# A recommendation tower on one core: twelve one-hot tables instead of ten, and a new order of products and layers

## What is computed

```python
e = jnp.stack([tbl_0[ids[:, 0]], ..., tbl_25[ids[:, 25]]], axis=1)       # 512 x 26 x 128
combined = jnp.concatenate([dense[:, None, :], e], axis=1)              # 27 fields
interactions = jnp.einsum('bfd,bgd->bfg', combined, combined)
z = concatenate([dense, interactions[:, iu, ju]], axis=1)               # iu, ju: pairs f < g
h = concatenate([z, dense], axis=1)
h = maximum(h @ W_top1 + b_top1, 0)                                     # 607 -> 512
h = maximum(h @ W_top2 + b_top2, 0)                                     # 512 -> 256
y = h @ W_top3                                                          # 256 -> 1
```

## Time and profile before

| | |
|---|---|
| Median of 3 runs | 120.84 us (120.73 to 121.73) |
| Profiled execution | 121.33 us |
| its span in the profile | 119.5 us |
| PE busy | 97.4 us (81%) |
| DVE, ACT, POOL busy | 74.1, 71.6, 67.1 us |
| mean granted TensorE clock | 0.986 of full |

### The profile page before, as it was taken

How to read it: one execution, slowest core, us unless ns; L and a number is a source line. 1 busy time by engine, 2 the same in 40 slices (tenths; PEclk the granted TensorE clock), 3 DMA queues, 4 the chain that set the end, 5 groups by cost and what they waited for, 6 DMA issues and landing times.

```text
span 119.5 us, 3462 instructions
## 1 busy us (share of the span) xinstructions
PE 97.4 (81%) x1494; PEld 78.9 (66%) x1494; DVE 74.1 (62%) x112; ACT 71.6 (60%) x137; POOL 67.1 (56%) x71
## 2 busy tenths in 40 slices
PE   0359999998999899689774949979997796498991
PEld 0147787784776677467563838969887795497760
DVE  2599799899979979992020890793079305184210
ACT  5449799999999997952322860792089110195101
POOL 2777777878687777777777677776740000000000
PEclk9999999999999999999999999999999999959999
DMA  2999974769958779721212222221220000000000
GB/s 69 240 333 348 331 246 110 250 85 293 389 167 302 230 171 334 278 69 37 59 44 71 52 54 62 49 69 47 56 59 5 0 0 5 5 0 0 0 5 1
DMA packets 5829, 14.72 MB, mean 123 GB/s; under 512 B 1707, under 2 KB 1707, under 8 KB 5686
## 3 DMA queue, kind: packets, MB, share of 16 engines
q1 hardware_dynamic: 3746, 10.28, 27.3%
q0 software_dynamic: 2048, 4.20, 12.7%
q10 hardware_dynamic: 20, 0.02, 0.1%
HBM read 14.50 MB, written 0.00 MB: 121 GB/s over the span
## 4 chain that ended last, share of the span: by engine, by line
PE 68%; DVE 20%; issue 8%; ACT 2%; ACTq 1%; DVEq 0%
PE gram_ps L475 17%; PE gram_ps L477 16%; PE gram_ps L521 9%; PE h_ps L546 8%; DVE zT L389 7%; DVE zT L386 7%; PE fill_ps L498 5%; PE h_ps L488 3%; PE h_ps L566 3%; DVE table_lo L409 2%; DVE featT L380 2%; PE fill_ps L576 2%; PE gram_ps L546 1%; DVE onehot L403 1%; ACT L319 1%
## 5 line engine op out<-in xcount | busy, mean ns | idle before, releaser
L263 POOL DMA_INDIRECT gathered<-tbl,ids_sb x64 | 66.3, 1035 | 20.7 <-issue 18.9
L475 PE MATMUL gram_ps<-onehot,table_hi 128*128 128x512 f32 x80 | 33.6, 420 | 5.5 <-DVE table_lo L409 3.8
L403 DVE TENSOR_TENSOR onehot<-h_ps,rowno 128x3072 fp32r<-128x3072 f32 (+1 forms) x11 | 33.6, 3060 | 3.0 <-PE h_ps L488 3.0
L477 PE MATMUL gram_ps<-onehot,table_lo 128*128 128x512 f32 x80 | 32.6, 407 | 0.0
L475 PEld LDWEIGHTS gram_ps<-onehot,table_hi 128*128 128x128 f32 x80 | 16.0, 199 | 10.5 <-issue 3.9
L386 DVE COPY zT<-gram_ps 32x128 f32<-32x128 f32 x32 | 9.1, 283 | 17.2 <-PE gram_ps L521 16.3
L521 PE MATMUL gram_ps<-featT 128*32 128x27 f32 x1024 | 13.1, 195 | 7.3 <-issue 4.9
L293 ACT ACTIVATE zT<-gram_ps 32x128 f32<-32x128 f32 x32 | 8.6, 270 | 16.0 <-PE gram_ps L521 15.4
L477 PEld LDWEIGHTS gram_ps<-onehot,table_lo 128*128 128x128 f32 x80 | 15.9, 199 | 3.2
L546 PE MATMUL h_ps<-zT,w_inter_sb 128*128 128x128 f32 x112 | 14.7, 280 | 2.5 <-DVE zT L389 2.5
L521 PEld LDWEIGHTS gram_ps<-featT 128*32 128x32 f32 x1024 | 10.9, 110 | 8.5 <-issue 5.9
(11 more groups left out here) (38 smaller groups left out, 65.0 us busy)
## 6 DMA issues: line engine op xcount, KB each, us to landing
table_sb<-tbl SPq DMA_DIRECT2D x10, 512.0 KB, 5.6
ids_all<-oh_ids SPq DMA_DIRECT2D x10, 256.0 KB, 4.9
gathered<-tbl,ids_sb POOLq DMA_INDIRECT x64, 4.2
w_inter_sb<-w_inter SPq DMA_DIRECT2D x1, 1024.0 KB, 7.6
w_dense_sb<-w_dense SPq DMA_DIRECT2D x1, 512.0 KB, 5.9
w_sb<-w SPq DMA_DIRECT2D x1, 512.0 KB, 9.0
dense_sb<-dense SPq DMA_DIRECT2D x1, 256.0 KB, 7.6
ids_sb<-ids SPq DMA_DIRECT2D x1, 52.0 KB, 1.9
```

Source lines behind the costliest of these rows:

```text
L263: pool.indirect_dma_start(out=gathered[:, t % ROW_BUFS, pos - FIRST_GATHERED, :], out_offset=None, in_=tables[table], in_offset=bass.Indir ...
L403: nc.vector.tensor_tensor(onehot[:, k % 2, c0:c1, :], ids_ps(k).unsqueeze(1).to_broadcast(of_chunks), rowno[:, c0:c1].unsqueeze(2).to_broa ...
L475: nc.tensor.matmul(lookup_ps(k), table_hi[:, k % SPLIT_BUFS, rows], onehot[:, k % 2, c, :], start=(c == 0), stop=False)
L477: last = nc.tensor.matmul(lookup_ps(k), table_lo[:, k % SPLIT_BUFS, rows], onehot[:, k % 2, c, :], start=False, stop=(c == RCHUNKS - 1))
```

## The change

`ONEHOT_TABLES` gains tables 18 and 20, so there are 12 lookups and 14 gathered fields; groups of gathered fields have 4, 4, 4 and 2 members. Fills (1,2), (1,3), (2,0) and (2,1) are put behind lookups. Both layers of tile t use one bank: `h1_ps`, `h2_ps` and a fill bank for tiles 0, 1, 2. `h1` has two buffers. PE's order is new: products of all tiles first, with layer 1 of tiles 0 and 1 between them; then second layers of tiles 0 and 1 and the first of tile 2; then the last tile in halves of 64 samples. `BLOCK` puts the quarters of a tile that DVE and ACT copy first into the first half. The functions with `_half` are new, `hidden1_last_half` goes. The scores are written into `denseT`.

```diff
-ONEHOT_TABLES = (0, 1, 3, 6, 8, 11, 12, 14, 15, 16)
+ONEHOT_TABLES = (0, 1, 3, 6, 8, 11, 12, 14, 15, 16, 18, 20)
-GROUPS = [range(p, p + GROUP) for p in range(FIRST_GATHERED, FEATS, GROUP)]
+GROUPS = [range(p, min(p + GROUP, FEATS)) for p in range(FIRST_GATHERED, FEATS, GROUP)]
+BLOCK = (0, 2, 1, 3)
-AFTER_LOOKUP = [[], [(0, 0)], [(0, 1)], [(0, 2)], [(0, 3)], [(1, 0)], [(1, 1)], [], [], []]
+AFTER_LOOKUP = [[], [(0, 0)], [(0, 1)], [(0, 2)], [(0, 3)], [(1, 0)], [(1, 1)], [(1, 2)], [(1, 3)], [(2, 0)], [(2, 1)], []]
-        h1 = sb("h1", [P, N1, P])
+        h1 = sb("h1", [P, 2, N1, P])
+        def layer_ps(t):
+            return (h1_ps, h2_ps, fill_ps[0])[t]
+        def layer1_half_ps(half, n):
+            return product_ps(LAST - 1)[:, half * BANK + n * HALF:half * BANK + (n + 1) * HALF]
+        def layer2_half_ps(half, n):
+            return (fill_ps[1], h1_ps)[half][:, n * HALF:(n + 1) * HALF]
+            def layer1_half(half):
+                pe.wait_ge(z_dve, 2 * ZCOPIES * LAST + (half + 1) * ZCOPIES)
+                pe.wait_ge(z_act, 2 * ZCOPIES * LAST + (half + 1) * ZCOPIES)
+                b0 = LAST * P + half * HALF
+                for n in range(N1):
+                    for c in range(ZCHUNKS):
+                        last = nc.tensor.matmul(layer1_half_ps(half, n), w_inter_sb[:, c, n * P:(n + 1) * P],
+                                                zT[:, c, b0:b0 + HALF],
+                                                start=False, stop=(c == ZCHUNKS - 1), skip_group_check=True)
+                last.then_inc(h1_psum_half, 1)
+            def layer2_half(half):
+                if half == 0:
+                    fills_read(1)
+                    pe.wait_ge(h1_ready, N1 * (LAST + 1))
+                else:
+                    pe.wait_ge(h2_ready, N2)
+                    pe.wait_ge(h1_act, N1)
...
             def layer2(t):
-                if t > 0:
-                    pe.wait_ge(h2_ready, N2 * t)
...
+                pe.wait_ge(h1_ready, N1 * (t + 1))
```

The end of the vector engine's order, the last tile's part on it and the scores:

```diff
             hidden1(2)
-            products_to_zT(3, 0)
-            products_to_zT(3, 1)
-            hidden1(LAST)
-            scores(1, 0, LAST * P)
-            scores(0, LAST * P, P)
+            hidden1_first_half()
+            hidden2_first_half()
+            scores(0, 0, LAST * P)
+            scores(1, LAST * P, P)
```

More of the change, by code:

```diff
@@ L148, in tower @@
         h2_psum = sem("h2_psum")
+        h2_psum_half = sem("h2_psum_half")
+        h2_half_dve = sem("h2_half_dve")
+        h2_half_act = sem("h2_half_act")
         h2_ready = sem("h2_ready")
@@ L308, in hidden2 @@
                 for n in range(N2):
-                    nc.scalar.activation(h2[:, n, t * P:(t + 1) * P], h2_ps[:, n * P:(n + 1) * P], ACT.Relu,
+                    nc.scalar.activation(h2[:, n, t * P:(t + 1) * P], layer2_ps(t, n), ACT.Relu,
                                          bias=b2_sb[:, n:n + 1]).then_inc(h2_ready, 1)
@@ L556, in layer2, with layer3 @@
                     pe.wait_ge(w2_in, 16)
-                if t > 0:
-                    pe.wait_ge(h2_ready, N2 * t)
[L559 to L568, removed]
-                last.then_inc(h2_psum, 1)
[L571 to L574, removed]
+                pe.wait_ge(h1_ready, N1 * (t + 1))
+                for n in range(N2):
+                    for k in range(N1):
+                        last = nc.tensor.matmul(layer2_ps(t, n), w2_sb[:, k, n * P:(n + 1) * P],
+                                                h1[:, t % 2, k, :], start=(n == 0 and k == 0), stop=(k == N1 - 1),
+                                                skip_group_check=True)
+                last.then_inc(h2_psum, 1)
+            def layer3(part, first, count):
+                pe.wait_ge(h2_ready, N2 * LAST)
+                if part == 1:
+                    pe.wait_ge(h2_half_dve, N2)
+                    pe.wait_ge(h2_half_act, N2)
                 for k in range(N2):
-                    last = nc.tensor.matmul(fill_ps[bank][0:1, 0:count], w3_sb[:, k:k + 1], h2[:, k, first:first + count],
+                    last = nc.tensor.matmul(score_ps(part)[0:1, 0:count], w3_sb[:, k:k + 1], h2[:, k, first:first + count],
                                             start=(k == 0), stop=(k == N2 - 1))
@@ L628, in _ @@
                 layer1(2, n)
[L629 to L632, removed]
-            layer2(2)
[L634 to L639, removed]
+            layer2(1)
+            layer1_dense_half(0)
+            layer1_dense_half(1)
+            layer1_half(0)
+            layer1_half(1)
+            layer2(2)
+            layer2_half(0)
+            layer2_half(1)
+            layer3(0, 0, LAST * P)
+            layer3(1, LAST * P, P)
 def first_layer_layout(w1):
```

182 lines of the change are left out of this document (107 added, 75 removed).

## The result

| | before | after |
|---|---|---|
| Median of 4 runs | 121.09 us (120.73 to 121.73) | 126.23 us (125.16 to 126.61) |
| Profiled execution, its span | 121.33, 119.5 us | 126.37, 124.5 us |
| First product starts | 58.54 | 67.73 |
| Last product ends | 104.05 | 98.24 |
| Last copy ends | 117.96 | 122.93 |

The ratio is 1.040, with a 95% interval of 1.032 to 1.049. The forecast was 128.5 us in 122.0 to 131.0. Whatever the kernel, some executions are longer by a few per cent; the ratios and intervals here, and the mean of old12b, use only the others (two each for `again`, whole12b, old12b and new10b), while the traces of `again`, whole12b, whole12c and new10b are of longer ones.

A forecast was written before the change was run, and what follows sets the result against it. DVE was taken to pace the lookups, PE's work and idle time the rest. Lookups to 68.1, 31.8 to the last product, 25.9 after and 1.54 store gave 127.3 us span, 128.5 us forecast, range 122.0 to 131.0.

The forecast's parts named there:

- Direction and bound: Whole kernel: slower, chance 0.86; DVE paces the lookups, PE's work plus its idle time sets the second stage.
- the waits for copies: PE's second-stage waits for DVE and ACT copies, about 5.9 us, go; no new wait that PE meets.
- narrower range of 125.5 to 130.5: Forecast's own range: 3.3 to 3.8 us a block, half-width instruction 0.10 to 0.12, lookups 9.1 to 11.3; chance 0.67.
- cheap halves: Rival, last tile: a 64-column matmul with new weights takes about 0.06 us, 6.3 us go, 122.2 us; chance 0.09.
- Two lookups, +10.2 us: Lookup stage: one more pair at the distance of lookups 6 to 8, 10.15 us; bounds 9.1 to 11.3 us.
- Stalls, 7.7 us: PE's products: waits for instruction blocks total 7.7 us against 4.94 before; 5.9 to 9.0 us by time per block.
- the 6 to 9 us that the prediction named as its sign: Products: idle time ending by issue, five to seven times, 255 instructions from end to end, would show the prediction right.
- the blocks of the prediction: PE's instructions arrive in blocks of 254, 3.6 us from entry to next arrival; first boundary about 176 instructions into the products.
- Halves, +6.3 us: Last tile: 112 instructions of 64 columns at 0.116 us, 13.0 us, replace 56 of 128 at 0.12, 6.7 us.
- The sum: Span 127.3 us: lookups to 68.1, 31.8 to the last product, 25.9 after it, 1.54 for the store.
- Clock: Rival: two stretches of product stalls bring the lower clock, each costing 1.2 us or so, 131 us; chance 0.12.

The follow-up runs named there:

- again: The new kernel unchanged, run again on the same chip and in the same rounds as whole12c: ratio to before 1.038.
- whole12b: The new kernel with the halves undone, last tile whole through both layers in the second fill bank, on another chip: ratio to before 1.013.
- old12b: The kernel before with twelve one-hot tables, its order and whole last tile kept: 127.03 and 127.38 us, where before had 121.0 beside it.
- new10b: The new order with the ten tables of before, two h1 buffers and the last tile whole: 116.06 and 117.69 us, ratio to before 0.970.
- whole12c: The new kernel with the last tile whole, on the first chip at a later time, beside the unchanged new kernel: ratio to before 0.996.
- wide: The new kernel with each half of the last tile's first layer computing all 128 columns: 125.55 us, before beside it 120.43.
- twice: The new kernel with each product matmul issued twice into the same place, 2048 more matmuls and weight loads: 156.49 us.

## Why the prediction was right, step by step

**Direction and bound.** Right. PE's work and its stalls set the second stage, and the waits for copies went away as said, with none in their place. The size was not as good: the forecast was 7.7 us above before (128.5 against 120.84), and the measured difference is 5.1. The narrower range of 125.5 to 130.5 holds the time too. But the range as stated also took in cheap halves (122.2 us), so the time by itself does not show that the mechanism was right; the rows of the halves and of the stalls do.

**Two lookups, +10.2 us.** 9.2 us. The term was taken from a pair with a full fill behind one lookup; fill (1,3) has two transposes now, its copy took 0.42 us instead of 0.73, and lookup 9 began at once; from lookup 8 to lookup 10 it is 49.13 to 58.79, 9.66 us. It lies within the bounds given (9.1 to 11.3), at the low one.

**Stalls, 7.7 us.** 5.6 us in the first trace, a little under the 6 to 9 us that the prediction named as its sign, and 6.8 in a later one of the same kernel. The places were right, all six: the blocks of the prediction, counted on from the 176th instruction, end with a stall in parts (0,3), (1,1), (1,2), (2,2), (3,1) and (3,3), and the stalls of the trace stand in the same parts. The sizes were too large by 0.35 us on average, partly because the work between them was larger: 25.6 us without stalls where the sum had 24.1. A first-layer quarter between products takes up to 1.1 us (84.77 to 85.76 and 87.63 to 88.72 from start to start) and not 0.96, while eight matmuls in a longer row take 0.9. Inside a block that has a stall, more work only takes the place of the stall: the two terms erred in opposite ways, and the product window came out within 0.6 us. The time of a block was about right too, 3.56 and 3.83 us in the two windows above against the 3.6 taken.

**Halves, +6.3 us.** Right in the mechanism: 112 instructions at 0.112 are 12.5 us, and 56 at 0.112 would be 6.3; whole12c shows 6.1 us in the trace and 5.2 us in the ratios. The prediction had 13.0 less 6.7. Both prices were too high, 0.116 and 0.12 for 0.112, since the 0.12 was a row's duration with its modelled end and not a distance between starts; that the difference of 6.3 us was met so closely is luck, as the two errors cancel. The weight load as the cause rests on wide (the columns do not matter up to 128), on the estimate of 0.054 us for 64 columns alone, and on the small products, which rule out a price of 0.11 us for just any instruction. A shorter weight load at 64 columns was not tried, so it is argued from these and not shown by an edit of its own.

**The sum.** 127.3 us of span, measured 124.5 (123.1 to 124.5 in the four runs). Lookups gave 1.0 us of the 2.8 too much, the product window 0.6 (31.2 against 31.8), the part behind it 1.2 (24.7 against 25.9, where a second layer took 1.8 us and not 1.95, a first layer 3.57 and not 3.84).

**Clock.** The rival of stretches at the lower clock was priced at about 1.2 us for each. They did not show in the first four runs (mean granted clock 1.0 in each), but one did in `again`, where `layer1(1, 2)` and `(1, 3)` took 2.86 us instead of 1.98 behind a stall of 2.20, with a granted clock of 0.67 of full. It is worth about a microsecond from run to run, and what decides in which run it falls stayed open. So did the reason why a stall at the same place took 1.38 us in one run and 2.20 in another.

**Where the gain went.** The change consists of three parts with a price each, on top of each other: twelve tables alone +6 us (old12b), the new order and banks about -6 us (-5 us for whole12b beside it, nearly -7 for whole12c, on another chip), halves +5 to +6 us. The Trainium skill's "mostly hidden" for block boundaries ("Runtime: NRT & Kernel Launch", "Instruction fetch mechanics") does not hold for these products: 5.6 us here, and 16.5 us in twice. The Trainium skill's rule for a weight load, the number of its columns divided by 1.2 in ns ("TensorE: Matmul & The Clock Gate", "LDWEIGHTS (loading the stationary operand)"), gives an estimate of 107 ns for 128 columns, which the 0.112 us agree with.

## What to carry to other kernels

Splitting a tile to overlap the tail costs a second set of weight loads when each matmul has its own 128 columns of weights: 64 moving columns took as long as 128, so look first whether the copies can lie beside another tile's layer. Where many tiny matmuls stand in a row, count instructions: some 255 of PE's per 3.4 to 4.1 us is what came through here, from one stall end to the next, and larger matmuls placed between them took the place of stalls. Price each part of a change by itself; here an order that was worth some 6 us was hidden behind two tables and a split that cost about eleven.

## What the runs showed of the hardware that was not expected

Blocks of 257 and 256 instructions took 3.7 and 3.5 us at 0.81 and at half of TensorE's clock alike, and every stall of this kind ended 2.15 to 2.90 us after a packet of the instruction queue had started. And wide's 64 matmuls of 128 columns took 7.15 us, to the hundredth what 64 of 64 columns took; I had expected 0.5 us more for them.
